# A gated cross-attention and FFN block: channels on partitions throughout, two chunks' attention in place in PSUM, one folded transform

## The reference

```python
x = x + tanh(g_xattn) * wkv(w, u, k=layernorm(x), v=ctx)
x = x + tanh(g_ffn) * ffn(layernorm(x))

# wkv, along the tokens t of each batch and channel (here without its running maximum, which only guards the range)
y_t = (sum_(s<t) exp(w*(t-1-s) + k_s) v_s + exp(u + k_t) v_t) / (the same sums without v)

# ffn
x = fwht(x * SU_ug) / 64                        # Walsh-Hadamard transform over 256 channels
up, gate = x @ W_up.T * a, x @ W_gate.T * b     # 256 -> 1024
x = fwht(silu(gate) * up * SU_dp) / 64          # over 1024
x = x @ W_down.T * c                            # 1024 -> 256
```

## Time and profile before

| | |
|---|---|
| median of 3 runs | 125.83 us (125.78 to 126.65) |
| the profiled execution's span | 124.1 us |
| TensorE busy | 100.7 us, 81% |
| VectorE busy | 83.9 us, 68% |
| ScalarE busy | 63.1 us, 51% |
| GpSimd busy | 57.4 us, 46% |
| read from HBM, written | 5.59 MB, 1.05 MB |

### The profile page before, as it was taken

The page is one execution under the profiler, slowest core; times in us unless marked ns, Lnnn a source line. Parts: engine busy times, 40 slices in busy tenths (PEclk is TensorE's granted clock), DMA queues, the critical chain, the costliest instruction groups (busy, mean ns, idle before and its releaser), DMA issues. The chain is left out here.

```text
span 124.1 us, 2050 instructions
## 1 busy us (share of the span) xinstructions
PE 100.7 (81%) x745; PEld 95.4 (77%) x745; DVE 83.9 (68%) x166; ACT 63.1 (51%) x133; POOL 57.4 (46%) x71
## 2 busy tenths in 40 slices
PE   0058415983679989999998949999999999999991
PEld 0057305853479889798997949999989999999990
DVE  0567999899999998994699667597864331223202
ACT  4276580693194566849928947224253442524400
POOL 4227491969756667822427454224532233242420
PEclk9999995599657999999999999999999999999999
DMA  3999991000000000000000000200000200000202
GB/s 91 243 320 387 350 344 68 0 0 3 0 5 3 0 0 0 0 5 0 0 0 5 0 3 0 85 0 8 0 0 0 85 5 0 0 0 21 69 0 85
DMA packets 6027, 6.77 MB, mean 55 GB/s; under 512 B 321, under 2 KB 5727, under 8 KB 6017
## 3 DMA queue, kind: packets, MB, share of 16 engines
q1 hardware_dynamic: 6017, 6.64, 16.7%
HBM read 5.59 MB, written 1.05 MB: 53 GB/s over the span
## 5 line engine op out<-in xcount | busy, mean ns | idle before, releaser
L368 POOL TENSOR_TENSOR HL<-H,HH 128x256 fp32r<-128x256 f32 x32 | 25.6, 801 | 37.0 <-ACT HH L454 36.8
L459 ACT ACTIVATE S<-UG,VT 128x256 f32<-128x256 f32 x32 | 15.1, 473 | 31.1 <-PE UG L761 31.1
L626 DVE SCALAR_TENSOR_TENSOR H<-S,ALPHA,UG 128x256 f32<-128x256 f32 x32 | 15.1, 473 | 18.7 <-ACT S L459 18.7
L761 PE MATMUL UG<-FH,WTH 128*128 128x256 f32 x128 | 21.2, 289 | 0.0
L761 PE MATMUL UG<-FH,WTL 128*128 128x256 f32 x128 | 20.8, 285 | 0.0
L761 PE MATMUL UG<-FL,WTH 128*128 128x256 f32 x128 | 20.6, 283 | 0.0
L761 PEld LDWEIGHTS UG<-FH,WTH 128*128 128x128 f32 x128 | 18.1, 195 | 0.2
L761 PEld LDWEIGHTS UG<-FH,WTL 128*128 128x128 f32 x128 | 17.9, 195 | 0.0
L761 PEld LDWEIGHTS UG<-FL,WTH 128*128 128x128 f32 x128 | 17.7, 192 | 0.0
L775 PE MATMUL OD<-MH,HH 128*128 128x256 f32 x56 | 16.4, 293 | 0.0
L775 PE MATMUL OD<-ML,HH 128*128 128x256 f32 x56 | 15.8, 283 | 0.0
(11 more groups left out here) (103 smaller groups left out, 190.3 us busy)
## 6 DMA issues: line engine op xcount, KB each, us to landing
WN<-in_w_gate SPq DMA_DIRECT2D x2, 512.0 KB, 7.8
DN<-in_w_down SPq DMA_DIRECT2D x2, 512.0 KB, 7.9
WN<-in_w_up SPq DMA_DIRECT2D x2, 512.0 KB, 8.9
out<-X SPq DMA_DIRECT2D x3, 256.0 KB, 2.1
X<-in_x SPq DMA_DIRECT2D x2, 256.0 KB, 5.7
V<-in_ctx SPq DMA_DIRECT2D x2, 256.0 KB, 7.0
X<-in_x SPq DMA_DIRECT2D x1, 512.0 KB, 10.6
V<-in_ctx SPq DMA_DIRECT2D x1, 512.0 KB, 9.3
```

Of the source, the lines that this page charges most:

```text
L368: pool.tensor_tensor(HL[:, q % JT, :], H[:, q % RING, :], HH[:, q % JT, :].bitcast(F32), ALU.subtract).then_inc(h_lo, 1)
L459: act.activation(S[:, q % RING, :], fill(("up", q))[:, 0:GT], ACT.Silu, scale=VT[:, V_SGATE + j:V_SGATE + j + 1]).then_inc(silu_ready, 1)
L626: dve.scalar_tensor_tensor(out=H[:, q % RING, :], in0=S[:, q % RING, :], scalar=ALPHA[:, j:j + 1], in1=fill(("up", q))[:, GT:2 * GT], op0= ...
L761: a = pe.matmul(fill(item)[:, m * GT:(m + 1) * GT], w[:, m, j, t, :], f[:, g % 2, t, :], start=(n == m == t == 0), stop=(n == 2 and t == C ...
```

## The change

- **Layout.** The host hands x over twice: with tokens on partitions for the first layer norm's statistics and keys (X), and with channels on partitions (XT). ctx comes with channels on partitions and one padding column per batch, the parameters as columns, half of W_gate and W_up (blocks 4 to 7) turned, W_down with the hidden channels on partitions. The residuals, the attention's result, the FFN's input and the output all have channels on partitions. `values`, `y` and `turn` are gone, and so are four of the eight `w` and their `w_rest`. The output leaves in that layout, too. `down` now multiplies with MH and ML as the stationary operand and gives channels on partitions.
- **In place in PSUM.** For chunks 0 and 1 (HELD) Exp of the keys, its product with the values, the mix, the estimate and the Newton step all lie in the one bank OD. Their scans use an unpadded decay D0 and a clearing of three columns. For chunks 2 and 3 EA and V in SBUF hold the same.
- **One folded transform.** The second layer norm's mean is taken out by the transform's matrix itself: AT is the Hadamard matrix with the signs SU_ug, minus its column means (`signs`, `center`). The transform works on x1 directly. The variance is that of the transform's result: `square`, a sum over channels by a matmul with ONES, Ln and Exp on ScalarE (`rstd2`), one correcting step on VectorE (`root`), and a scaling (`f_scaled`), then the split. For chunks 0 and 1 (WHOLE) the transform is 4 matmuls on plain float32 operands; for 2 and 3 x1 is split into XH and XL, 8 fp32r matmuls.
- **W_down.** Two levels of butterflies (8 operations, all on GpSimd) in place of three (12), the third level by accumulation, on plain float32 operands of 512 columns, two matmuls for each of four `m`; `d` and its rounding are gone, `m_rest` takes the rounded part off in PSUM. The scale of the output is applied by VectorE when the output is added.
- **Slots.** Four passes of 256 columns, as before. LAG is 4 in place of 6. The last four `down` are done in two halves, all four for the first 128 channels and then for the others. The output's sum alternates between the banks OD and KZ.
- **Loads.** The list is x0, parameters, constants, steps, x1, half of W_gate, W_down, half of W_up, ctx0, xt0, the other halves, x2, ctx1, xt1, ctx2, xt2: 6.5 MB.

```diff
...
-LAG = 6
+LAG = 4
+WHOLE = (0, 1)
...
+HELD = (0, 1)
...
+    0: [("keys", 3), ("m_rest", 1)],
+    4: [("m", 2), ("fwht", 1)],
+    5: [("m_rest", 2), ("ones", 1), ("m", 3)],
...
+        def exps(g):
+            if g in HELD:
+                return OD[:, :].rearrange("p (t b q) -> p t b q", t=CT, b=GB)
+            return EA[:, g - len(HELD), :, :, 1:PAD]
...
+        def states(tile, g):
+            if g in HELD:
+                return tile[:, 0:CT * GT].rearrange("p (t b q) -> p t b q", t=CT, b=GB)
...
+        def multiply_values(eng, g, done):
+            eng.wait_ge(ctx_in[arrival(g)], 16)
+            if g in HELD:
+                eng.wait_ge(den_ready, g + 1)
             else:
-                eng.wait_ge(flown[t], 2 * step)
...
-            sp.dma_start(STEP[0:32 + CT, :, :].rearrange("p t n -> p (t n)"), steps).then_inc(step_in, 16)
+            sp.dma_start(STEP[:, :, :].rearrange("p t n -> p (t n)"), steps).then_inc(step_in, 16)
+            load_x(1)
+            load_w(0, 0)
+            sp.dma_start(DN[:, :, :], w_down).then_inc(down_in, 16)
+            load_w(1, 0)
             load_ctx(0)
-            def load_w(m, h):
-                j = slice(h * JT // 2, (h + 1) * JT // 2)
...
+                elif name == "sum":
+                    pool.wait_ge(squared, CT + g)
+                    if g > 1:
+                        pool.wait_ge(v_full, g)
+                    pool.tensor_tensor(FSUM[:, :], FSQ[:, 0, :], FSQ[:, 1, :], ALU.add).then_inc(summed, 1)
...
+                elif name == "signs":
...
+                    for o in range(CT):
+                        for t in range(CT):
+                            act.activation(GG[:, o, t, :], HN[:, :] if o and t else HAD, ACT.Copy, scale=VT[:, V_SUG + t:V_SUG + t + 1]).then_inc(signs, 1)
...
+                elif name == "square":
...
+                        act.activation(FSQ[:, :, :], fx, ACT.Square).then_inc(squared, 1)
+                    else:
+                        for t in range(CT):
+                            act.activation(FSQ[:, t, :], fx[:, t, :], ACT.Square).then_inc(squared, 1)
+                elif name == "rstd2":
+                    act.wait_ge(v_full, g + 1)
+                    if g == 0:
+                        act.wait_ge(eps_set, 1)
+                    act.activation(RR[:, :], VB[:, 0:GT], ACT.Ln, bias=EPSC[:, 0:1]).then_inc(log_ready, 1)
+                    act.wait_ge(log_ready, g + 1)
+                    if g:
+                        act.wait_ge(e_ready, 3 * g)
+                    act.activation(RR[:, :], RR[:, :], ACT.Exp, scale=-0.5).then_inc(rr_ready, 1)
+                elif name == "f_hi":
+                    for t in range(CT):
+                        act.wait_ge(f_scaled, CT * g + t + 1)
+                        act.activation(FH[:, g, t, :], FN[:, t, :], ACT.Copy).then_inc(f_hi, 1)
...
+                if g in HELD:
+                    dve.tensor_tensor_scan(tile[:, 1:CT * GT + 1], D0[:, :, :, :].rearrange("p t b q -> p (t b q)"), steps,
+                                           0.0, ALU.mult, ALU.add).then_inc(done, 1)
+                    dve.wait_ge(done, 2 * g + 1)
+                    dve.memset(tile[:, P:CT * GT:P], 0.0).then_inc(done, 1)
...
+                    dve.wait_ge(centers, 1)
+                    for o in range(CT):
+                        dve.tensor_tensor(AT[:, o, :, :], GG[:, o, :, :].bitcast(F32),
+                                          FX[:, o * P:(o + 1) * P].unsqueeze(1).broadcast_to([P, CT, P]), ALU.subtract).then_inc(at_ready, 1)
...
+                    dve.wait_ge(y_ready, g + 1)
+                    dve.wait_ge(tanh_gate, 1)
+                    dve.wait_ge(xt_in[arrival(g)], 16)
+                    xg = XT[:, g, :, :].rearrange("p t (b q) -> p (t b) q", q=P)
+                    dve.scalar_tensor_tensor(out=xg, in0=lanes(values(g)), scalar=TG[:, 0:1], in1=xg, op0=ALU.mult, op1=ALU.add).then_inc(x1_ready, 1)
...
+                elif name == "root":
+                    var = VB[:, 0:GT]
+                    dve.wait_ge(rr_ready, g + 1)
+                    dve.scalar_tensor_tensor(out=var, in0=var, scalar=EPS * C, in1=RR[:, :], op0=ALU.add, op1=ALU.mult).then_inc(e_ready, 1)
+                    dve.wait_ge(e_ready, 3 * g + 1)
+                    dve.tensor_tensor(var, var, RR[:, :], ALU.mult).then_inc(e_ready, 1)
+                    dve.wait_ge(e_ready, 3 * g + 2)
+                    dve.scalar_tensor_tensor(out=RB[:, :], in0=var, scalar=3.0, in1=RR[:, :], op0=ALU.subtract, op1=ALU.mult).then_inc(e_ready, 1)
+                elif name == "f_scaled":
+                    dve.wait_ge(e_ready, 3 * g + 3)
+                    if g:
+                        dve.wait_ge(f_hi, CT * g)
+                        dve.wait_ge(f_lo, g)
+                    for t in range(CT):
+                        dve.scalar_tensor_tensor(out=FN[:, t, :], in0=FX[:, t * GT:(t + 1) * GT], scalar=-0.5, in1=RB[:, :],
+                                                 op0=ALU.mult, op1=ALU.mult).then_inc(f_scaled, 1)
...
+            def out_of(g, t):
+                xg = XT[:, GROUPS[g][0]:GROUPS[g][-1] + 1, t, :]
+                dve.wait_ge(down_full, g + 1 if g < LAST else LAST + 1 + t)
+                dve.scalar_tensor_tensor(out=xg, in0=total(g, t).rearrange("p (g n) -> p g n", n=GT), scalar=OUTS[:, t:t + 1], in1=xg,
+                                         op0=ALU.mult, op1=ALU.add).then_inc(out_ready, 1)
...
+                elif name == "m":
+                    item = ("m", g)
+                    wait_bank_free(pe, item)
+                    wait_shared(pe, "fly", *(4 + 2 * i + g % 2 for i in range(2)))
+                    pe.wait_ge(neg_ready, 1)
+                    for i in range(2):
+                        had = HN[:, :] if i and g // 2 else HAD
+                        n = 4 * i + 2 * (g % 2)
+                        a = pe.matmul(fill(item)[:, :], had, DN[:, n:n + 2, :].rearrange("p j c -> p (j c)"), start=(i == 0), stop=False, skip_group_check=True)
+                    a.then_inc(m_full, 1)
+                elif name == "m_rest":
+                    pe.wait_ge(m_hi, M_HI.index(g) + 1)
+                    pe.wait_ge(ni_ready, 1)
+                    pe.matmul(fill(("m", g))[:, :], NI[:, :], m_part(MH, g), start=False, stop=True, skip_group_check=True).then_inc(m_left, 1)
...
+                elif name == "fwht":
+                    if g == 0:
+                        pe.wait_ge(at_ready, CT)
+                    else:
+                        pe.wait_ge(f_scaled, CT * g)
+                    if g in WHOLE:
+                        pe.wait_ge(x1_ready, g + 1)
+                        for t in range(CT):
+                            for o in range(CT):
+                                i = pe.matmul(FX[:, o * GT:(o + 1) * GT], AT[:, o, t, :].bitcast(F32), XT[:, g, t, :],
+                                              start=(o == t == 0), stop=(t == CT - 1), skip_group_check=True)
+                    else:
+                        pe.wait_ge(x_hi, X_HI.index(g) + 1)
+                        for n, part in enumerate((XH, XL)):
+                            if n:
+                                wait_shared(pe, "x_lo", g)
+                            for o in range(CT):
+                                for t in range(CT):
+                                    i = pe.matmul(FX[:, o * GT:(o + 1) * GT], AT[:, o, t, :], part[:, t, :],
+                                                  start=(n == o == t == 0), stop=(n == 1 and t == CT - 1), skip_group_check=True)
...
+                elif name == "ones":
                     if g:
-                        pe.wait_ge(x1_ready, g)
-                    for b in range(GB):
+                        pe.wait_ge(e_ready, 3 * g)
+                        pe.wait_ge(summed, g)
+                        i = pe.matmul(VB[:, 0:GT], ONES[:, :], FSUM[:, :], start=True, stop=True)
+                    else:
...
-                for name, g in PE_STAGES.get(q, []):
-                    if name == "w_rest":
-                        take_hi_off(("w", g))
-                    elif name in ("w", "d", "m"):
-                        prep((name, g))
-                    else:
-                        stage(name, g)
                 if q >= LAG:
                     down(q - LAG)
+                for name, g in PE_STAGES.get(q, []):
+                    stage(name, g)
             for q in range(SLOTS - LAG, SLOTS):
-                down(q)
+                pe.wait_ge(h_lo, q + 1)
+                down_part(q, 0)
+            for q in range(SLOTS - LAG, SLOTS):
+                down_part(q, 1)
...
+        "x": np.ascontiguousarray(np.asarray(inputs["x"]).transpose(1, 0, 2)),
+        "xt": turned(inputs["x"]),
+        "ct": np.pad(turned(inputs["ctx_2048"]).reshape(P, NG, CT, GB, P), ((0, 0),) * 4 + ((1, 0),)),
+        "vecs": np.ascontiguousarray(np.concatenate([columns, np.broadcast_to(gates, (P, 2))], axis=1)),
```

(2 more changed lines are left out.)

983 lines of the change are left out of this document (519 added, 464 removed).

## The result

The changed kernel takes 118.98 us (median; before, in the same comparison, 125.81), a ratio of 0.947 with a 95% interval of 0.942 to 0.952. A second comparison, later, gave 118.65 and 0.943 (0.938 to 0.948). The ratios leave out executions over 1.5% longer than the fastest of the same kernel (one of 198 us here), the medians don't, so the two can differ by more than a per cent. The forecast was 118.0, with 113 to 122 as its range.

A forecast was written before the change was run, and what follows sets the result against it. TensorE's own work was taken to bound the loop, but not the start. `up(6)` at 50.0, then 59.0 of `up` and `down`, 3.1 side work, 1.5 idle give 113.6; with the tail span 116.3, plus 1.7 median 118.0, range 113 to 122.

The forecast's parts named there:

- In place in PSUM: Attention of chunks 0 and 1: two-input VectorE operations with one input in PSUM take 0.47 and 0.68 us.
- Plain fp32: Transforms of chunks 0 and 1, `ones` and `m`: unrounded products take 0.48 us per 256 columns, double at the low clock.
- cheap fp32: Rival: unrounded fp32 products cost only 0.12 us per 256 columns, giving 110 us; chance 0.13 (109 to 114).
- Loads: Start: w_down complete at 12.0 us, the first ctx at 14.1, xt0 at 14.9, priced at 2.76 us per MB.
- Behind x1: From chunk 0's x1 at 21.1 us to the first `up` at 31.8, with VectorE's chunk 1 last at 29.1.
- the other side: Rival: clock stays low from the first transform to `up(6)`, making the kernel slower, up to 138 us; chance 0.03.
- Slots 0 to 5: From the first `up` to `up(6)`: Silu(0) ends at 38.5 us, `up(6)` starts at 50.0 with two `down` done.
- ScalarE as the bound: Rival: ScalarE's queue in slots 3 to 6 and its blocks hold TensorE up, 122 to 123 us; chance 0.14.
- The rest: From `up(6)` to TensorE's end: 59.0 us of `up` and `down`, 3.1 of side work, 1.5 idle.
- The 0.4 at `up(8)`: In the loop: 0.4 us of TensorE idle time at `up(8)`, waiting for ScalarE's block in slot 5.
- 0.5 for what I can't place: Behind `up(6)`: 0.5 us of TensorE idle time allowed without a place, part of the 1.5 idle.
- The tail: Behind TensorE's end at 113.6: last addition 0.43 us, store and end 2.24, span 116.3, median 1.7 above.

The follow-up runs named there:

- SBUF run: The changed kernel with the attention of chunks 0 and 1 kept in SBUF instead of in place in the PSUM bank: 127.19 us, ratio to before 0.997.
- six traces with this start: Profiled executions of the changed kernel (twice) and four edits of it, all with the same program up to the first `up`, which starts at 31.64 to 34.21 us.
- run with the pauses filled: The changed kernel with 21 dummy fp32r products in TensorE's idle stretches ahead of chunk 0's transform: 117.31 us, ratio to before 0.934.
- HL on VectorE: The changed kernel with the low part of the last slot's hidden values made by VectorE instead of GpSimd: 118.13 us, ratio to before 0.938.
- split of x1: The changed kernel with chunks 0 and 1 transformed from two rounded parts by fp32r products instead of plain float32: 120.9 us, ratio to before 0.957.
- Sum early: The changed kernel with VectorE adding a finished chunk to the output before that slot's hidden values, at slots 12, 20 and 28: 117.13 us, ratio 0.926.

## Why the prediction held, point by point

**In place in PSUM: right, and it carries the change.** 0.48 and 0.70 us against the 0.47 and 0.68 that I priced. What I did not price is its absence: the SBUF run shows that the new layout, with one engine doing all butterflies, gains nothing without it.

**Plain fp32: right.** In the chain four products of 256 columns take 1.73 and four of 512 1.72, thus 0.43 per 256 columns, a little under my 0.48, and 0.94 at the low clock as I had it. The rival *cheap fp32* is out, as the row at 44.35 shows. The low clock for the first transform was priced rightly, but its reason ("TensorE was idle before") is not what this trace shows: the pace was low from the first product on.

**Loads: off by 0.75.** The context landed at 14.85, not 14.1. In the six traces with this start the product with it begins at 13.64 to 15.86, so the price was good and this execution a little unlucky. Normalising chunk 1 took 2.02, not 1.64, with GpSimd at work beside it (the same two instructions for chunk 0, at 6.14 with GpSimd idle, take 0.73). So x1 at 22.01 for 21.1. (My 0.15 for a clearing came from no row; it takes 0.06.)

**Behind x1: the step that failed.** I let the low clock end with the transform and put m(0) at 1.84 and the first `up` at 31.8. m(0) took 2.98 of the chain, so that `ones`, not VectorE's chunk 1, was last, and the first `up` came at 33.16. The run with the pauses filled gave 31.23, with x1 0.3 later, and shows that this was the clock. When the pace rises is not fixed by the program: in the six traces the clock goes to 1.00 for good at 25.7 to 28.8 us. In one of them, HL on VectorE, it does so as the transform ends, just as I had assumed, and the first `up` is at 32.09:

```profile
22.36 3.62 PE L861 MATMUL FX<-XT,AT 128*128 128x256 f32 x8 [0.69 <-DVE XT L727]
...
25.82 1.88 PE L829 MATMUL UG<-DN,HI 128*128 128x512 f32 x4
```

So the step is wrong as a rule and right by chance in some executions. The profiled one is the mild case of my rival *the other side*: the low pace ended by about 28 us, and it never reached slots 0 to 5.

**Slots 0 to 5: right, with an offset.** Silu(0) ended at 39.38 for 38.5, `up(6)` at 50.57 for 50.0, two downs ahead of it. My reason for `up(4)` was wrong: H(0) was ready at 39.89, ahead of TensorE, which had been busy since 35.1 with `keys`, m_rest and `up(1)` to `up(3)` and ended `up(4)` at 41.92, not 40.6. The 1.3 us shrank to 0.6 because HL(0) no longer had to be waited for (0.25 in my walk) and because m, transform and `ones` were cheaper than priced (0.5). *ScalarE as the bound* did not come: behind the first `up` TensorE's timeline has no wait for ScalarE above 0.21 us. The split of x1 shows how near it is: one more copy of chunk 1 made a wait of 1.59.

**The rest: the size right, the place wrong.** Work 61.93 us for 62.1, idle 2.0 for 1.5. The 0.4 at `up(8)` did not occur, the 0.6 at the end did (111.74 and 112.43), and behind "0.5 for what I can't place" stood 1.57: the last chunk sums into both banks at once, OD was chunk 2's, and its addition stood behind the hidden values of slot 28. I had called VectorE's additions covered, or 0.9 if exposed in full; the queue order in front of them belonged to the price. "Sum early" took it away.

**The tail: right.** 2.8 us from TensorE's end to the end of the span for my 2.7, and the median 1.7 above the span.

The total came out 1.0 above the forecast, all of it span: 1.4 lost at the first `up`, 0.8 given back by `up(6)`, 0.3 lost behind it and 0.1 in the tail. With a start that varies by 2.6 us between executions, a forecast within 1.0 is partly luck.
